# Root mean squares kept in every partition: ones as the stationary, squares as 512 moving columns

## The reference

```
h = layernorm(x) * (1 + ca) + sa
xn    = norm1_w * h / sqrt(mean(h*h) + 1e-8)          # first RMS norm
left  = gelu(xn @ left_W + left_b)
right = rg_lru(conv4(xn @ right_W + right_b))          # two gate products, a scan over time
x1    = (left * right) @ out_W + out_b + h
x1n   = norm2_w * x1 / sqrt(mean(x1*x1) + 1e-8)        # second RMS norm
mlp   = (gelu(x1n @ up1_W + up1_b) * (x1n @ up2_W + up2_b)) @ down_W + down_b
x     = x + ga * (mlp + x1)
h     = layernorm(x) * (1 + cb) + sb
x     = x + gb * (moe(h) + h)                          # 8 experts, the best 2 of each token
```

## Time and profile before

| | us |
|---|---|
| median of 3 runs | 317.01 |
| lowest, highest | 315.55, 319.29 |
| the profiled execution's own time | 314.15 |
| its span in the trace | 312.3 |
| PE busy | 272.5 |
| DVE busy | 194.6 |
| ACT busy | 180.6 |

### The profile page before, as it was taken

The page is one execution under the profiler, slowest core; times in us unless marked ns, Lnnn a source line. Parts: engine busy times, 40 slices in busy tenths (PEclk is TensorE's granted clock), DMA queues, the critical chain, the costliest instruction groups (busy, mean ns, idle before and its releaser), DMA issues. The chain is left out here.

```text
span 312.3 us, 4371 instructions
## 1 busy us (share of the span) xinstructions
PE 272.5 (87%) x1556; PEld 229.8 (74%) x1556; DVE 194.6 (62%) x450; ACT 180.6 (58%) x290; POOL 115.6 (37%) x97
## 2 busy tenths in 40 slices
PE   0799999957999999959695979999999999999780
PEld 0685546346688888837563969999999999999770
DVE  4766719829736386474793576868586867675420
ACT  5167589763487239444142669494949494949000
POOL 6000000000133143337065800747474756565741
PEclk9999999976999999995759799999999999999995
DMA  7960000000005664502014955585848494727231
GB/s 233 386 198 0 2 1 0 0 0 2 0 0 205 203 167 88 202 20 105 20 65 124 274 177 166 163 235 152 247 150 248 140 260 138 218 21 200 22 42 26
DMA packets 32725, 38.25 MB, mean 122 GB/s; under 512 B 7988, under 2 KB 28332, under 8 KB 32684
## 3 DMA queue, kind: packets, MB, share of 16 engines
q1 hardware_dynamic: 26816, 29.90, 30.7%
q0 software_dynamic: 4928, 7.44, 10.6%
q10 hardware_dynamic: 956, 0.59, 0.7%
HBM read 31.96 MB, written 8.90 MB: 131 GB/s over the span
## 5 line engine op out<-in xcount | busy, mean ns | idle before, releaser
L1709 POOL DMA_INDIRECT out_x<-y_tok,meta x24 | 51.6, 2149 | 52.4 <-DVE y_tok L1581 46.2
L869 PE MATMUL bank<-w_hi,own 128*128 128x256 f32 x256 | 48.0, 285 | 1.8 <-DVE y_tok L1581 1.8
L847 PE MATMUL bank<-xe_hi,w_hi 128*128 128x320 f32 x128 | 40.4, 315 | 3.3 <-DVE xe_lo L1559 3.3
L1563 DVE TENSOR_TENSOR own<-own_raw,own 128x256 fp32r<-128x256 f32 x64 | 27.2, 425 | 24.8 <-ACT own L1139 20.1
L869 PEld LDWEIGHTS bank<-w_hi,own 128*128 128x128 f32 x256 | 40.4, 191 | 2.4 <-issue 2.0
L847 PE MATMUL bank<-xe_hi,w_lo 128*128 128x320 f32 x128 | 40.3, 315 | 0.0
L847 PE MATMUL bank<-xe_lo,w_hi 128*128 128x320 f32 x128 | 40.2, 314 | 0.0
L1133 ACT ACTIVATE own_raw<-bank,b1c 128x320 f32<-128x320 f32 x64 | 33.8, 529 | 9.9 <-PE bank L847 9.9
L869 PE MATMUL bank<-w_lo,own 128*128 128x256 f32 x128 | 36.2, 283 | 0.0
L1139 ACT ACTIVATE own<-own_raw 128x320 fp32r<-128x320 f32 x64 | 28.7, 460 | 0.0
L1700 POOL DMA_INDIRECT gb_rows<-gb_table,meta x24 | 24.9, 1037 | 8.9 <-issue 7.0
(11 more groups left out here) (211 smaller groups left out, 611.4 us busy)
## 6 DMA issues: line engine op xcount, KB each, us to landing
e_raw<-in_L_ffn_w SPq DMA_DIRECT2D x16, 1024.0 KB
x_rows<-in_L_attn_x SPq DMA_DIRECT2D x1, 2560.0 KB
xe_tok<-x_rows SPq DMA_DIRECT2D x8, 256.0 KB
raw_m<-in_L_attn_up_W SPq DMA_DIRECT2D x2, 768.0 KB, 9.6
x_tok<-in_L_attn_x SPq DMA_DIRECT2D x2, 512.0 KB, 5.1
out_x<-x_tok SPq DMA_DIRECT2D x1, 1024.0 KB
wmod<-in_L_wmod SPq DMA_DIRECT2D x1, 768.0 KB, 12.0
raw_m<-in_L_attn_down_W SPq DMA_DIRECT2D x1, 768.0 KB, 13.0
```

The source lines that it names most:

```text
L847: ins = nc.tensor.matmul(bank[b][:, 0:CAP], l, r, start=(c == 0 and t == 0), stop=(c == KD - 1 and t == 2))
L869: ins = nc.tensor.matmul(bank[b][0:n, 0:D], l, r, start=(c == 0 and t == 0), stop=(c == KE - 1 and t == 2))
L1563: nc.vector.tensor_tensor(own_lo[e % 2][:, f, :], own_raw[:, f % 4, 0:whole], own_hi[e % 2][:, f, 0:whole].bitcast(F32), ALU.subtract)
L1709: nc.gpsimd.indirect_dma_start(out_rows, bass.IndirectOffsetOnAxis(ap=ids[0:n, e, k, E:E + 1], axis=0), y_tok[e % 2][0:n, k, :], None, com ...
```

## The change

The ones, broadcast to 128x128, become the stationary and the squares the moving operand: 2 matmuls of 512 columns a chain, whose result is the sum of squares of each token in every partition, 128x512. ACT takes the root of the whole bank, DVE the reciprocal of the whole 128x512 in place, and `rms_apply` reads it from SBUF. The four `spread` products go, and with them their banks. The result lies in memory that is free at that time: two slices of `tmp` for the first norm, one of `tmp` and one of `ui` for the second.

```diff
-            def mean_square(key, hf, n):
+            def square_sum(key, hf, n):
                 b, ps = begin(key)
                 for dt in range(KD):
                     pe.wait_ge(square_done, KD * n + dt + 1)
-                    for j in range(TH):
-                        ins = nc.tensor.matmul(ps[:, j:j + 1], square[:, dt, hf * HT + j * P:hf * HT + (j + 1) * P], ones, ...)
-                end(ins, b)
-            def spread(key, hf):
-                b, ps = begin(key)
-                for j in range(TH):
-                    ins = nc.tensor.matmul(ps[:, j * P:(j + 1) * P], rinv[:, hf, j:j + 1].to_broadcast([P, P]), ident[:], ...)
+                    ins = nc.tensor.matmul(ps[:], ones.to_broadcast([P, P]), square[:, dt, hs[hf]], start=(dt == 0), stop=(dt == KD - 1))
                 end(ins, b)
...
-                until_drained(("rb", hf), 2)
+                pe.wait_ge(xn_done, KD * (hf + 1))
...
-            def mean_root(key, hf):
+            def mean_root(key, n):
                 b, ps = full(key)
-                nc.scalar.activation(rms[:, hf, :], ps[:, 0:TH], ACT.Sqrt, bias=eps_rms, scale=1.0 / D).then_inc(drained[b], 1)
+                nc.scalar.activation(rinv[n], ps[:], ACT.Sqrt, bias=eps_rms, scale=1.0 / D).then_inc(drained[b], 1)
...
-            def rms_inverse(key, hf, n):
+            def rms_apply(key, n, src, w):
+                hf = n % NH
                 until_drained(key)
-                nc.vector.reciprocal(rinv[:, hf, :], rms[:, hf, :]).then_inc(rinv_done, 1)
-            def rms_apply(key, hf, src, w):
-                b, ps = full(key)
+                st.link(nc.vector.reciprocal(rinv[n], rinv[n]))
                 ...
                 for dt in range(KD):
-                    ins = nc.vector.scalar_tensor_tensor(..., in1=ps[:], ...)
+                    nc.vector.scalar_tensor_tensor(..., in1=rinv[n], ...).then_inc(xn_done, 1)
...
-            rms_inverse(("ms", 0), 0, 1)
             ln_apply(x_tiles(1), xhat, 2).then_inc(xhat_done, 1)
             until_drained("vec")
-            rms_apply(("rb", 0), 0, ("xh", 2), "norm1_w")
+            rms_apply(("ms", 0), 0, ("xh", 2), "norm1_w")
             modulate("xh", 1, CA, SA)
...
             conv(0)
-            rms_inverse(("ms", 1), 1, 2)
             conv(1)
-            rms_apply(("rb", 1), 1, ("xh", 2), "norm1_w")
+            rms_apply(("ms", 1), 1, ("xh", 2), "norm1_w")
...
-                if n == 2:
-                    rms_inverse(("ms2", 1), 1, 4)
                 if n == 3:
-                    rms_apply(("rb2", 1), 1, ("out", 1), "norm2_w")
+                    rms_apply(("ms2", 1), 3, ("out", 1), "norm2_w")
                     m_lo(2)
```

More of the change, by code:

```diff
@@ L83, in adaln_block @@
     order = Order()
-    for key in ["cT", "mod_a", ("xh", 0, 0), ("xh", 0, 1), ("ms", 0), "vec", ("rb", 0), ("xh", 1, 0), ("xh", 1, 1)]:
-        order.take(key, drains=2 if key[0] in ("xh", "rb") else 1)
+    for key in ["cT", "mod_a", ("xh", 0, 0), ("xh", 0, 1), ("ms", 0), "vec", ("xh", 1, 0), ("xh", 1, 1)]:
+        order.take(key, drains=2 if key[0] == "xh" else 1)
     def take_side(side, hf):
@@ L92, in adaln_block @@
     take_side("left", 0)
-    order.take(("rb", 1), drains=2)
     def take_gates(hf):
@@ L110, in adaln_block @@
     order.take(("ms2", 0))
-    order.take(("rb2", 0), drains=2)
     def take_up(hf, m):
@@ L143, in adaln_block @@
     take_up(0, 3)
-    order.take(("rb2", 1), drains=2)
     take_up(0, 4)
@@ L222, in adaln_block @@
         rstd = new("rstd", [TT])
-        rms = new("rms", [2, TH])
-        rinv = new("rinv", [2, TH])
         before = new("before", [E, E])
@@ L271, in adaln_block @@
         v_tile = [tmp[:, 4, :], tmp[:, 5, :], v_more[:, 0, :], v_more[:, 1, :]]
+        rinv = [tmp[:, 10, :], tmp[:, 11, :], tmp[:, 4, :], ui[:, 0, HT:]]
         wmod = at("wmod", o_r1 + 4 * TB, [KD, GB * D])
@@ L354, in adaln_block @@
         mv_done, std_done, xhat_done = sem("mv_done"), sem("std_done"), sem("xhat_done")
-        square_done, rinv_done = sem("square_done"), sem("rinv_done")
+        square_done, xn_done = sem("square_done"), sem("xn_done")
         n_hi_done, n_lo_done = sem("n_hi_done"), sem("n_lo_done")
@@ L557, in mean_square @@
                     pe.wait_ge(square_done, KD * n + dt + 1)
-                    for j in range(TH):
-                        ins = nc.tensor.matmul(ps[:, j:j + 1], square[:, dt, hf * HT + j * P:hf * HT + (j + 1) * P], ones,
-                                               start=(dt == 0 and j == 0), stop=(dt == KD - 1 and j == TH - 1))
-                end(ins, b)
-            def spread(key, hf):
-                b, ps = begin(key)
-                for j in range(TH):
-                    ins = nc.tensor.matmul(ps[:, j * P:(j + 1) * P], rinv[:, hf, j:j + 1].to_broadcast([P, P]), ident[:],
-                                           start=True, stop=True)
+                    ins = nc.tensor.matmul(ps[:], ones.to_broadcast([P, P]), square[:, dt, hs[hf]], start=(dt == 0), stop=(dt == KD - 1))
                 end(ins, b)
@@ L594, in _ @@
             pe.wait_ge(consts_done, 2)
-            mean_square(("ms", 0), 0, 0)
+            square_sum(("ms", 0), 0, 0)
             pe.wait_ge(vec_in, 16 * len(names[0::2]))
@@ L598, in _ @@
             transposes("vec", lambda j: rows[0:NV, :], 1, NV)
-            pe.wait_ge(rinv_done, 1)
-            spread(("rb", 0), 0)
             pe.wait_ge(xhat_done, 2)
@@ L635, in _ @@
             side("right", 0, 0)
-            mean_square(("ms", 1), 1, 1)
+            square_sum(("ms", 1), 1, 1)
             side("left", 1, 0)
-            pe.wait_ge(rinv_done, 2)
-            spread(("rb", 1), 1)
             def gates(hf):
@@ L652, in out_products, with square_sum2 @@
                     whole_product(("out", hf, dt), 4, dt, y_all, hf)
[L654 to L659, removed]
+            def square_sum2(hf):
+                square_sum(("ms2", hf), hf, hf + 2)
             gates(0)
@@ L674, in _ @@
             out_products(0)
-            mean_square2(0)
-            spread2(0)
+            square_sum2(0)
             wm_ready(2)
@@ L765, in _ @@
             x_blocks("xr", 0, x_tok)
-            mean_square2(1)
+            square_sum2(1)
             up(0, 3)
-            spread2(1)
             up(0, 4)
@@ L1005, in _ @@
             squares(0, "out", 1)
-            mean_root(("ms2", 0), 0)
+            mean_root(("ms2", 0), 2)
             roots(1)
-            hi_of_n(0, ("rb2", 0))
+            hi_of_n(0)
             act.wait_ge(y_done, KH)
@@ L1064, in _ @@
                     keep_x(0)
-                    mean_root(("ms2", 1), 1)
+                    mean_root(("ms2", 1), 3)
                 if n == 3:
@@ L1068, in _ @@
                 if n == 4:
-                    hi_of_n(1, ("rb2", 1))
+                    hi_of_n(1)
                     keep_x(1)
@@ L1281, in rms_apply, with rms_lo @@
                 for dt in range(KD):
[L1282 to L1288, removed]
+                    nc.vector.scalar_tensor_tensor(out=xn[:, dt, hs[hf]], in0=hT[:, dt, hs[hf]], scalar=C(w, dt), in1=rinv[n],
+                                                   op0=ALU.mult, op1=ALU.mult).then_inc(xn_done, 1)
+                dve.wait_ge(xn_done, KD * (n + 1))
+            def rms_lo(hf, n):
                 for dt in range(KD):
@@ L1382, in _ @@
             x1_of(0)
-            rms_inverse(("ms2", 0), 0, 3)
-            rms_apply(("rb2", 0), 0, ("out", 1), "norm2_w")
-            rms_lo(("rb2", 0), 0, 1)
+            rms_apply(("ms2", 0), 2, ("out", 1), "norm2_w")
+            rms_lo(0, 1)
             recur(2)
```

6 lines of the change are left out of this document (3 added, 3 removed).

## The result

| | before | changed |
|---|---|---|
| median, us | 317.15 (4 runs) | 326.03 (4 runs) |
| lowest, highest | 315.55, 319.29 | 324.9, 327.05 |
| profiled execution, its span | 314.15, 312.3 | 326.62, 324.8 |

The ratio is 1.0328, 95% interval 1.0284 to 1.0371, and the medians are 8.9 us apart. These two don't quite agree: the medians alone give 1.028, while 1.0328 is 10.3 us. The 66 later runs of the kernel before, made for the experiments, on several chips with medians from 315.2 to 315.9, have one of 315.4 us together, with which the change costs 10.6 us. So the price is 9 to 10.6 us, and the four runs of before shown here were a little slow. Ratios and intervals leave out runs more than 1.5% above the fastest of their kernel, medians are of all runs.

The account below looks back on a forecast made before the run. TensorE, busy 272.5 of 312.3 us, was taken as the bound, with nothing later recovering losses. Terms 2.8 + 1.3 + 2.7 + 1.0 = 7.8 us gave 324.8 on the median; predicted 324.3, range 319.5 to 328.5.

Parts of the forecast that it names:

- Reciprocal, 3.5 us: DVE's reciprocal of 128x512 was estimated at 3.5 us from the small ones, with 2.5 and 4.0 as bounds.
- The first rival: The reciprocal streams like any other instruction, 0.7 us; sum -2.4 us, about 314.6 on the median; chance 0.10.
- Place A: First norm: reciprocal delays the right product, which then runs at half pace; gates begin at 36.7, not 33.89: +2.8 us.
- half pace behind the new gap: First norm: after 3 us without work TensorE runs the first two right products at half pace, 5.3 us in all.
- Second reciprocal of the first norm, 0: First norm, second half: 3.5 us on DVE hidden behind the 7.03 us of gates on TensorE; term 0.
- Place B: Second norm, first half: reciprocal ends at 70.4, where multiplication had begun at 68.97: +1.3 us (0.3 to 1.8).
- Place C: Second norm, second half: up(1, 0) waits for n_lo until 101.25 against 98.52 before: +2.7 us (1.6 to 3.4).
- Clock behind C: After the new 3.5 us gap ahead of up(1, 0), TensorE's granted clock may fall to 0.50: +1.0 us (0 to 3).
- Behind the gates nothing makes up for it: Behind the first norm's gates, a chain of TensorE, ACT and DVE was said to win back none of the +2.8 us.
- Sum against which time: The 7.8 us sum gives 322.0 on the profiled execution, 324.8 on the 317.01 median; 324.3 was predicted.
- Rival 2: Reciprocal slow but only partly shows: +1.0, +1.0 and +1.5 us, no clock fall; +3 us or less, about 320; chance 0.15.
- Rival 3: Forecast with a deeper clock fall: +3.5, +1.8, +3.2 and clock +3; +11.5 us, 328.5; chance 0.15.

Follow-up runs that it names:

- The filled gap: Changed kernel plus 2 fp32 matmuls of 512 columns without a use ahead of the first right product: ratio 1.0361 to the kernel before, 325.65 us.
- the second chain alone: Kernel before with only the chain of the first norm, second half, in the new form: ratio 0.996, 315.57 against 315.4 us.
- the fourth chain alone: Kernel before with only the chain of the second norm, second half, in the new form: ratio 1.0174, 320.78 against 315.4 us.
- the reciprocal earlier: Changed kernel with the reciprocal of the second norm, second half, moved back behind v_of(2) on DVE: ratio 1.0211 to the kernel before, 322.11 us.

## Why the prediction was right

The forecast was 324.3 us, +7.3 on the 317.0 shown; measured 326.03, +8.9 on 317.15 and +10.6 on the 315.4 of the later runs. The mechanism and all places were as forecast; every term of the sum but C was too small, and that the forecast came within 1.7 us of the time owes something to the runs of before that were shown, which were slow: from 315.4 it would have said 322.7.

- **Reciprocal, 3.5 us:** measured 3.35. Leaving it out took the whole loss away, so the term on which all hung is shown. The first rival (it streams in 0.7 us) falls. Its 2.4 us of gain were not there either when the reciprocal was left out: the ratio is 0.9966, and the medians of all runs are 0.3 us apart the other way.
- **Place A, +2.8:** measured 3.25. `xn` came as worked out (the right products at 25.87, worked out 26.05). The half pace behind the new gap, which only the durations show, was right in kind and too small: I gave it two matmuls and 5.3 us, it was 6.28. The filled gap bears it out in part, as said there. The pair of traces understates the step: where the gates begin varies with the pace, from 32.60 to 33.89 in five traces with the first norm as before (before is the latest of them) and from 36.88 to 37.14 in three with it as changed, 3.8 us apart on average.
- **Second reciprocal of the first norm, 0:** shown by the second chain alone.
- **Place B, +1.3:** measured 1.50 in the changed kernel and 1.50 to 1.56 alone. By the times alone it may cost more; that is open.
- **Place C, +2.7:** measured 2.35. The wait of 3.19 us is in the stated 3 to 3.6.
- **Clock behind C, +1.0 (0 to 3):** the term that was mis-sized most. From up(1, 0) to down(0) takes 2.72 us at full clock; it took 2.54 more in the changed kernel, and the clock fell with the fourth chain alone too (1.70 more), and even behind gaps of 2.09 and 1.83 us (1.69 and 1.54 more). I had halved the term for the chance that it would not fall. With 2.5 the sum is 9.3 us, and with the 3.8 at place A and the 1.5 and 2.35 at B and C 10.2, against the 8.9 to 10.6 measured.
- **"Behind the gates nothing makes up for it":** right. The 1.7 us that came on top there in the pair of traces are the low clock behind the modulation products, which before happened to lack. That the loop over the experts "has no break" was not exact: TensorE waits up to 3.1 us in it for `xe_lo`. It made up for nothing, 140.8 us in both traces.
- **Sum against which time:** I took the sum to the median and stayed 0.5 under it. The profiled pair would have said +12.5, because the execution of before was among its fastest; the four runs of before were above the 315.4 of the later ones, which was luck for the number.
- **Rival 2** (partly hidden, +3) is excluded by the interval. **Rival 3** (a deeper fall of the clock, 11.5) is too large as a whole, but its 3 us for the clock is nearer to the 2.54 than my 1.0.

## What to carry to other kernels

A reciprocal on DVE is paid by the element, so it belongs on the smallest form of the data; spreading before it gives it 128 times the elements and took it from 0.17 to 3.35 us, and the spread that is saved, 1.05 or 2.08 us on TensorE, does not pay for it. The same form can pay where the function is ACT's, which costs 0.69 us for 128x512 out of a bank, and its table load is put behind the chain: 1.6 us of one chain here, at the edge of what the times could tell. A delay costs its length where TensorE waits already (place B); in front of a TensorE that had been busy it costs the new wait and the low clock behind it, 2.35 + 2.54 us at place C; and it costs nothing at all beside 7 us of other work. And one trace of each kernel can mislead: here 12.5 us between the traces were 9 to 10.6 in the times.

## What the runs showed of the hardware that was not expected

- **The reciprocal's rate.** 3.35 us for 512 elements is 6.2 ns an element. The Trainium skill ("VectorE: DVE Perf Modes", First, the fixed hardware budget) speaks of a repeat count of 8; at the 0.96 GHz that it gives the measured step is 6.0 cycles, so a price of 8 cycles, 4.3 us, would be too high. The measurement decides.
- **DVE beside GpSimd.** The same in-place `tensor_scalar` of 128x512 took 0.42 us three times and 1.48 us once. GpSimd's timeline of that kernel shows a subtraction in the same time, from 90.95 to 92.25:

```profile
90.95 1.30 POOL L1623 TENSOR_TENSOR v_lo<-v_more,v_hi 128x512 fp32r<-128x512 f32 x1 [4.41 <-ACT v_hi L989]
```

  The same holds for `m_lo(2)`: 1.76 us in the changed kernel, where it begins after GpSimd's second subtraction has ended (102.09), and 2.73 us with the reciprocal earlier, where a subtraction is under way:

```profile
100.50 1.57 POOL L1629 TENSOR_TENSOR v_lo<-v_more,v_hi 128x512 fp32r<-128x512 f32 x1 [1.16 <-ACT v_hi L989]
100.96 2.73 DVE L1297 TENSOR_TENSOR wm_lo<-raw_m,wm_hi 128x1536 fp32r<-128x1536 f32 x1
```

  The reciprocal itself ran beside two such subtractions (98.33 and 100.80 in the changed kernel) and took its usual 3.34. So the slow instruction had also moved others out of GpSimd's way, and its removal won less at C than its length: 1.86 us by the instruction, of which `m_lo(2)` gave 0.99 back (2.75 instead of 1.76). The Trainium skill ("SBUF — State Buffer", SBUF: two separate sides) says that the two engines share one port pair as an exclusive lock, for which a vector instruction contends if it is in a two-port mode or, against a GpSimd instruction that reads SBUF, has two inputs in SBUF, and that the one that starts first keeps it for its whole instruction. These rows agree: both late instructions began while a subtraction was running, and were late by a little less than what was left of it (1.06 of 1.20 and 0.97 of 1.11 us), while the reciprocal, with one input, was not. `m_lo` has two inputs. The `tensor_scalar` has one, so by that rule it must have been in a two-port mode, which its 0.42 us, against 0.68 for two-input instructions of that size, allows but does not show.
- **The clock after short gaps.** In the dense work at place C the granted clock fell to about 0.50 behind gaps of 3.17 to 3.20 us in three traces, and behind gaps of 2.09 and 1.83 us in one trace each, while behind one of 2.23 us it did not (the up products there ran at full pace). So the length of the gap alone doesn't decide it in this range, and one trace of each can't say how often it falls.
